# Output product one slot later, between the sixth and seventh transposition, and the first route weights transposed inside the first expert unit

## What is computed

```python
# x: 16 batches x 128 tokens x 128; y: 16 x 77 x 96; 16 heads of 8
q = layernorm(x) @ Wq.T + bq;  k, v = split(y @ Wkv.T + bkv)
att = softmax(q k / sqrt(8));  out = (att v) @ Wo.T + bo
x = x + tanh(g_xattn) * out
cur = layernorm(x)                       # 2048 tokens x 128
for r in range(4):                       # 4 rounds, 4 experts of width 512, top 2
    logits = cur @ Wg[r] + bg[r]
    cw = softmax over the best two of four, 0 for the others
    cur = cur + sum_e cw[e] * (gelu(cur @ W1[e] + b1[e]) @ W2[e] + b2[e])
x = x + tanh(g_ffn) * cur
```

## Time and profile before

| | |
|---|---|
| median of 3 runs (lowest, highest) | 456.02 us (455.89, 456.13) |
| the profiled execution | 455.4 us, of which its span 453.6 us |
| PE busy | 445.1 us, 98% of the span |
| DVE, ACT, POOL busy | 80%, 79%, 15% |
| granted TensorE clock | 1.000 over the span |
| slots 0 to 15 (12.1 to 85.6 us), the turn into the experts (to 96 us), expert units (the rest) | |

### The profile page before, as it was taken

The page is one execution under the profiler, slowest core; times in us unless marked ns, Lnnn a source line. Parts: engine busy times, 40 slices in busy tenths (PEclk is TensorE's granted clock), DMA queues, the critical chain, the costliest instruction groups (busy, mean ns, idle before and its releaser), DMA issues.

```text
span 453.6 us, 8799 instructions
## 1 busy us (share of the span) xinstructions
PE 445.1 (98%) x2856; PEld 354.8 (78%) x2856; DVE 362.1 (80%) x729; ACT 359.4 (79%) x742; POOL 70.2 (15%) x109
## 2 busy tenths in 40 slices
PE   8999999999999999999999999999999999999996
PEld 6666777778787888788878887888788878888885
DVE  6998989887978688868876888688768876887776
ACT  5777877696969779877987798779887888788883
POOL 7939884323000000000000000000000000000000
PEclk9999999999999999999999999999999999999999
DMA  6690000130021101300120022002200310023001
GB/s 168 194 206 15 1 10 10 61 129 3 0 93 30 66 1 36 153 0 1 72 117 1 1 80 108 0 2 100 88 0 1 135 53 1 0 95 117 25 0 46
DMA packets 12892, 25.18 MB, mean 56 GB/s; under 512 B 4615, under 2 KB 8496, under 8 KB 10800
## 3 DMA queue, kind: packets, MB, share of 16 engines
q1 hardware_dynamic: 9408, 22.23, 14.0%
q0 software_dynamic: 2784, 2.18, 2.6%
q10 hardware_dynamic: 656, 0.23, 0.2%
HBM read 22.82 MB, written 1.18 MB: 53 GB/s over the span
## 4 chain that ended last, share of the span: by engine, by line
PE 91%; DVE 4%; issue 2%; ACT 1%; DMA 1%; POOL 0%; SPq 0%; POOLq 0%; DVEq 0%
PE ps L1419 13%; PE ps L1421 13%; PE ps L1420 13%; PE ps L1408 12%; PE ps L1407 12%; PE ps L1406 12%; PE ps L1286 4%; PE ps L1308 2%; PE ps L1272 2%; PE ps L1314 2%; DVE least L899 1%; DMA x_sb<-in_x_dram 1%; PE ps L1373 1%; ACT g_sb L808 1%; PE ps L1321 1%
## 5 line engine op out<-in xcount | busy, mean ns | idle before, releaser
L955 DVE TENSOR_TENSOR h_lo<-g_sb,h_hi 128x512 fp32r<-128x512 f32 x256 | 169.9, 687 | 70.7 <-ACT h_hi L815 70.6
L808 ACT ACTIVATE g_sb<-ps,cols 128x512 f32<-128x512 f32 x256 | 174.4, 694 | 36.0 <-PE ps L1408 35.5
L815 ACT ACTIVATE h_hi<-g_sb 128x512 fp32r<-128x512 f32 x256 | 155.9, 640 | 0.0
L1419 PE MATMUL ps<-h_hi,w_hi 128*128 128x512 f32 x252 | 101.0, 401 | 0.1
L1406 PE MATMUL ps<-x_hi,w_hi 128*128 128x512 f32 x256 | 99.8, 390 | 0.0
L1408 PE MATMUL ps<-x_hi,w_lo 128*128 128x512 f32 x256 | 99.6, 389 | 0.0
L1407 PE MATMUL ps<-x_lo,w_hi 128*128 128x512 f32 x256 | 99.6, 389 | 0.0
L1421 PE MATMUL ps<-h_hi,w_lo 128*128 128x512 f32 x252 | 98.4, 390 | 0.0
L1420 PE MATMUL ps<-h_lo,w_hi 128*128 128x512 f32 x252 | 98.1, 389 | 0.0
L1419 PEld LDWEIGHTS ps<-h_hi,w_hi 128*128 128x128 f32 x252 | 47.3, 188 | 13.1 <-issue 2.7
L1408 PEld LDWEIGHTS ps<-x_hi,w_lo 128*128 128x128 f32 x256 | 48.1, 188 | 10.0
(11 more groups left out here) (126 smaller groups left out, 376.7 us busy)
## 6 DMA issues: line engine op xcount, KB each, us to landing
cwb_even<-cw_rows SPq DMA_DIRECT2D x8, 1024.0 KB, 5.4
cwb_odd<-cw_rows SPq DMA_DIRECT2D x8, 1024.0 KB, 4.7
w_hi<-in_L_ffn_W_dram POOLq DMA_DIRECT2D x2, 1024.0 KB, 10.3
w_in<-in_L_ffn_W_dram SPq DMA_DIRECT2D x1, 1024.0 KB, 5.4
x_sb<-in_x_dram SPq DMA_DIRECT2D x3, 256.0 KB, 5.3
out_dram<-xn SPq DMA_DIRECT2D x3, 256.0 KB, 2.5
ctxT<-in_ctx_dram SPq DMA_DIRECT2D x3, 115.5 KB, 5.1
v_st<-v_sb SPq DMA_DIRECT2D x14, 19.2 KB
```

The costliest lines, as they stand in the source:

```text
L808: nc.scalar.activation(g_sb[:, k, :], ps[:, k, :], ACT.Gelu_apprx_tanh, bias=b1_c[:, e * NF + k:e * NF + k + 1]).then_inc(gelu_done, 1)
L815: nc.scalar.activation(h_hi[:, u % 2, k, :], g_sb[:, k, :], ACT.Copy).then_inc(hi_done, 1)
L955: nc.vector.tensor_tensor(h_lo[:, u % 2, k, :], g_sb[:, k, :], h_hi[:, u % 2, k, :].bitcast(F32), ALU.subtract).then_inc(lo_done, 1)
L1419: mm(yb, w2_hi[:, w], hh, start=k == 0, stop=False)
```

## The change

Three edits. (1) The output product moves: PE computes `project_o(b-3)` in slot b, after the sixth transposition (after `transpose_probs(b, 1)`), instead of `project_o(b-2)` after the tenth; slot 15 holds both `project_o(12)` in the new place and `project_o(13)` in the old one. (2) DVE's `add_residual(b-3)`, which needs that product, moves from the start of slot b to behind `normalise_o(b-2)`; `add_residual(13)` moves to behind `weights(0)` in slot 15. (3) `transpose_weights(0)` moves from the end of slot 15 into `up(0)`, behind its first block, and its copy `move_cwT(0)` on ACT to behind `gelu(0, 0)`. Nothing is added or removed.

```diff
--- before.py
+++ after.py
@@ -286,7 +286,6 @@
 
         XT_AT = (10, 13)
         LG_AT = (13, 15)
-        CWT0_AT = 15
         ROUTER_SLOT = 15
         K_AT = {8: 3}
         V_AT = {10: 3}
@@ -320,12 +319,11 @@
                 next_job(("K", K_AT[b]), "act")
             if b in V_AT:
                 next_job(("V", V_AT[b]), "act")
-            if b == CWT0_AT:
-                next_job(("CWT", 0), "cwT")
             if b == 0:
                 job(("V", 2), "dve", 7)
                 job(("K", 2), "dve", 6)
                 last_early.update({6: ("K", 2), 7: ("V", 2)})
+        next_job(("CWT", 0), "cwT")
         next_job(("CWT", 1), "cwT")
         next_job(("XT", 2), "act")
         reads(("K", 0), "act")
@@ -784,9 +782,8 @@
                 exponentials(b, 1)
                 if b in XT_AT:
                     move_cur(XT_AT.index(b))
-                if b == CWT0_AT:
+                if b == ROUTER_SLOT:
                     gate(0)
-                    move_cwT(0)
                 if b in XN_AT:
                     move_xn(XN_AT[b])
                 if b in BUSY and b + 1 < B:
@@ -825,6 +822,7 @@
                 high(u, 3)
 
             gelu(0, 0)
+            move_cwT(0)
             gelu(0, 1)
             high(0, 0)
             gelu(0, 2)
@@ -1115,14 +1113,14 @@
             moments(0, 1)
             for b in range(B):
                 c, r = b // TC + 1, b % TC
-                if b >= 3:
-                    add_residual(b - 3)
                 if b >= 2:
                     invert_sums(b - 2)
                 if b + 1 < B:
                     smallest(b + 1, 1)
                 if b >= 2:
                     normalise_o(b - 2)
+                if b >= 3:
+                    add_residual(b - 3)
                 if b + 1 < B:
                     smallest(b + 1, 0)
                 if b + 1 < B:
@@ -1133,6 +1131,7 @@
                     moments(*MOMENTS[b])
                 if b == ROUTER_SLOT:
                     weights(0)
+                    add_residual(B - 3)
                 if b in NORMALISE:
                     normalise(NORMALISE[b])
                 if b == 0:
@@ -1158,7 +1157,6 @@
                     nc.vector.tensor_copy(wg_w[:, :, 0:E], wg_in[:, :, :]).then_inc(wg_split, 1)
             invert_sums(B - 2)
             normalise_o(B - 2)
-            add_residual(B - 3)
             weights(1)
             invert_sums(B - 1)
             normalise_o(B - 1)
@@ -1394,12 +1392,12 @@
                 tr(CWT(q), cw[:, 0:n, :, :].rearrange("p i e t -> p (i e t)"),
                    ident[:, :]).then_inc(job_mm if q < 2 else cwT_done, 1)
 
-            def up(u):
+            def up(u, blocks=range(NF)):
 
                 e, i = u % E, u // E
                 c = i % NC
                 pe.wait_ge(x_split, i + 1)
-                for k in range(NF):
+                for k in blocks:
                     w = slice(e * F + k * P, e * F + (k + 1) * P)
                     if u >= 1:
                         pe.wait_ge(gelu_done, NF * (u - 1) + k + 1)
@@ -1479,6 +1477,8 @@
                     scores(b + 1)
                 transpose_probs(b, 2)
                 transpose_probs(b, 1)
+                if b >= 3:
+                    project_o(b - 3)
                 if b in XN_AT:
                     transpose_xn(XN_AT[b])
                 if b in XT_AT:
@@ -1486,8 +1486,8 @@
                 if b in LG_AT:
                     logits(LG_AT.index(b))
                 transpose_probs(b, 0)
-                if b >= 2:
-                    project_o(b - 2)
+                if b == B - 1:
+                    project_o(B - 3)
                 if b in Q_AT:
                     project_q(Q_AT[b])
                 if b in K_AT:
@@ -1496,15 +1496,15 @@
                     project_v(V_AT[b])
                 if b >= 1:
                     weigh_values(b - 1)
-                if b == CWT0_AT:
-                    transpose_weights(0)
                 if b == 0:
                     project_v(2)
                     project_k(2)
             pe.wait_ge(w_split, 16)
             for h in range(2):
                 pe.wait_ge(below_done[h], B)
-            up(0)
+            up(0, range(0, 1))
+            transpose_weights(0)
+            up(0, range(1, NF))
             weigh_values(B - 1)
             transpose_weights(1)
             project_o(B - 2)
```

## The result

| | before | after |
|---|---|---|
| median of 8 runs each (lowest, highest) | 455.95 us (455.62, 456.23) | 457.38 us (457.21, 457.61) |
| span of the profiled execution | 453.6 us | 455.6 us |
| PE, DVE busy | 445.1, 362.1 us | 445.8, 363.6 us |

The change costs 1.43 us: ratio 1.0032, 95% interval 1.0021 to 1.0043. That is inside the range, on its slower side, and within 0.1 of rival B (457.3), not of the forecast (456.8).

What follows compares the result with a forecast made beforehand. The end was taken to hang on the chain from slot 14's sums through DVE's routers and ACT's list to `down(0)`'s third block, not PE. Slots -0.22 plus way +1.02 gave +0.80: median 456.8 us, range 456.0 to 457.6.

Steps and rivals of the forecast that it cites:

- rival B: Slots get slower too: additions between score reads cost a 0.25 signal, ACT-bound slots win nothing; +0.3, 457.3; chance 0.35.
- The way to `down(0)`: From slot 14's sums to the third block of `down(0)`: three delays arrive whole at PE, +1.02 us.
- (a): Slot 15: `add_residual(12)` before the router waits for the product after the sixth transposition; router starts 0.61 us later.
- (b): `add_residual(13)` moves from behind the second router to ahead of it, and nothing covers it: +0.26 us.
- (c): `move_cwT(0)` leaves ACT's slot 15 and enters its expert list between two `gelu`: +0.15 us.
- The slots: All slots up to slot 14: gains and losses from the moved product and additions sum to -0.22 us.
- Slots 2, 5, 8 and 9: Projection behind the tenth transposition waits for an ACT copy; 0.07 us can be won in each, four slots -0.27.
- Plain slots 6, 7, 12: DVE takes the place of ACT's wait; with a 0.20 us signal the next scores come 0.03 later per slot, +0.09 together.
- Slots 3 and 4: DVE is late; PE's 0.42 us wait for `oT_sb` goes but becomes a wait for `subtract`: scores +0.10 us.
- Slots 10 and 11: Same pattern as in slots 3 and 4, with DVE less late: +0.08 us.
- A: PE's time lands whole: slots are PE-bound, no wait follows, about -2.1 there, 454.9 in all, faster; chance 0.08.
- C: Routers not that late: product comes earlier or addition slips beside, 0.26 us instead of 0.61 in slot 15; 456.5; chance 0.15.

Runs made afterwards that it cites:

- second profile: The whole change run once more on another chip, same order of instructions, against the kernel before: 457.31 against 455.88 us, +1.43 (ratio 1.0027).
- slot 15 alone: Kernel before with product and additions in their new places only in slot 15, add_residual(13) ahead of router(1), no edit (3): 456.84 against 456.03 us, +0.81.
- shortened additions: Changed kernel with add_residual of batches 0 to 11 cut to 8 of 128 columns: 456.37 against 455.78 us for the kernel before, +0.59.
- slots 5 and 14: Kernel before with output product and addition in their new places in slots 5 and 14 only (batches 2 and 11): 455.52 against 455.88 us, -0.36.

## Why the prediction was right and wrong

**What bounds the kernel:** right. The sum of what moved before the third block of `down(0)`, 1.42 us in the second profile, is the measured 1.43, and what follows that block kept its length.

**The way to `down(0)`, forecast +1.02:** right, +1.02 and +1.03 in the two profiles. Terms (a) and (b), forecast 0.87: 0.87 in slot 15 alone and 0.88 with edits 1 and 2. Term (a) by itself: from the first transposition of slot 15 to the router 81.97 - 80.91 = 1.06 before and 83.53 - 81.87 = 1.66 after:

```profile
81.87 1.14 PE L1284 MATMUL ps<-ident,below 128*128 128x128 f32 x6 [0.28 <-ACT probT L723]
...
87.49 0.28 PE L1392 MATMUL ps<-ident,cw 128*16 128x128 f32 x1 [0.36 <-DVE lg L1001]
```

0.60 against the forecast 0.61. Term (b) 0.26 (86.80 to 87.06 on DVE), against 0.26. Term (c), forecast 0.15: 0.15 and 0.17. Edit (3)'s worth of nothing was right, and by the mechanism given: PE waits for the same late logits behind the first block (0.36 at 87.49).

**The slots, forecast -0.22:** wrong, +0.40 in two profiles (+0.24 where slot 4's stall is missing). This is where the missed 0.6 us lie; that the sum still fell inside the range is owed to the range, which took in case B. By term:

- *Slots 2, 5, 8 and 9*, forecast -0.27, measured -0.01, +0.04, +0.03, 0: +0.06 in all. It is the term that was sized most wrongly, by 0.33. The step that failed is "0.07 can be won": it took `xnT` as ready at the old time. But the product also stands ahead of the transposition of `xn`, and lasts as long as the wait that it fills. PE in the change, slot 5:

```profile
35.76 0.87 PE L1284 MATMUL ps<-ident,below 128*128 128x128 f32 x6
36.47 0.39 PE L1319 MATMUL ps<-wo_t,oT_sb 128*128 128x128 f32 x2
36.69 0.63 PE L1234 MATMUL ps<-ident,xn 128*128 128x128 f32 x4
```

and ACT:

```profile
37.36 0.60 ACT L695 ACTIVATE xnT<-ps 128x512 f32<-128x512 f32 x1
```

  `xnT` starts 37.36 - 34.99 = 2.37 after the scores, 36.53 - 34.19 = 2.34 before the change. Nothing in front of the last wait had become earlier, so nothing could be won behind it; 0.03 came on top. Slot 9 has no transposition of `xn`. There the projection does start 0.07 earlier, 2.29 us after the scores (56.11 - 53.82 in the second profile) instead of 2.36 (55.15 - 52.79), but it starts from a wait:

```profile
56.11 0.30 PEld L1248 LDWEIGHTS ps<-xnT,wq_t 128*128 128x128 f32 x2 [0.23 <-ACT probT L725]
```

  and `weigh_values` follows 1.06 behind it instead of 0.99, so that nothing is left.
- *Plain slots 6, 7, 12*, forecast +0.03 each, measured +0.04, +0.08, +0.07: +0.19 instead of +0.09. The step is "so I take 0.20": from the end of `subtract` to the scores it took 0.23 in slot 7 by the rows above, and the transpositions start 0.76 behind the scores instead of 0.73. Rival B's condition was a signal of over 0.22. That DVE takes the place of ACT's wait was right and is shown by the shortened additions; the addition's own cost was right too (0.27 from its start to the next instruction, 46.44 to 46.71, against 0.26).
- *Slots 3 and 4*, forecast +0.10, measured +0.10 with edits 1 and 2 alone, +0.25 to +0.26 in the three other profiles with both in the new order. The scores of slot 5, without edit 3 and in the change:

```profile
34.70 0.34 PEld L1275 LDWEIGHTS ps<-k_st,q_st 32*128 32x128 f32 x8 [0.33 <-issue]
```
```profile
34.99 0.34 PEld L1270 LDWEIGHTS ps<-k_st,q_st 32*128 32x128 f32 x8 [0.49 <-issue]
```

  What the further 0.16 us of "issue" are stays open: `subtract` ended 0.38 before the scores instead of 0.23, and no engine's end goes with them. The shortened additions, in the same new order, don't show them (4.55).
- *Slots 10 and 11*, forecast +0.08, measured 0 and +0.09. *Slot 13*, forecast -0.22, measured -0.20, and -0.23 where it alone was changed. *Slot 14*, forecast 0, measured 0. All right.

**The rivals.** B is nearest to what happened: nothing was won where ACT is waited for, and up to slot 14 it had +0.3, measured +0.24 to +0.40. Its signal of 0.25 did not come, only 0.22 to 0.23, at the very edge of its condition; and the upper part of the loss, slot 4's 0.16, is a stall that no case contained, so some of the nearness of its 457.3 is luck. It had 0.35 and the forecast 0.42: the forecast took a middle value for the signal between two bounds and went on with it as if it were known. A is out: the 0.22 us landed whole in one slot of twelve. C is out by slot 15 alone. "Slower by over 0.2%" had 0.43 and was the outcome.

**The signs.** The seventh transposition has no idle time before it: so. Plain slots 3.93 to 4.0: 3.98 to 4.02, with PE idle before the scores for 0.33, though the profile names no releaser where the forecast had DVE L906. The first router step 0.6 after `normalise_o`'s end, behind an addition that waits for PE: 83.53 - (82.63 + 0.29) = 0.61, with [0.34 <-PE ps L1319] before the addition:

```profile
82.63 0.29 DVE L922 TENSOR_TENSOR oT_sb<-ps,rT_sb 128x128 f32<-128x128 f32 x1
83.26 0.35 DVE L928 SCALAR_TENSOR_TENSOR x_sb<-ps,tgates,x_sb 128x128 f32<-128x128 f32 x1 [0.34 <-PE ps L1319]
```

ACT's `th` before the table load 0.65 later: not so. It is at 89.40, and without the later start (0.33) and slot 2's stall (0.22) it is 89.40 - 87.56 - 0.55 = 1.29 later; the 0.64 too much are what the slots were off by. The third block of `down(0)` at 96.8: at 98.03, of which 0.33 is the later start of that profile and 0.22 slot 2's stall.

## What to carry to other kernels

Work put into a wait of PE is only free if what it needs from the other engines is free too: here 0.22 us of PE per slot went into a real wait, and the addition that belonged to it moved from DVE's idle time into the stretch between two reads that the next slot waits for, where 0.12 us of it cost PE 0.13. Before a gain behind a wait is counted, ask what the waited-for work itself waits for: if the moved piece now stands ahead of it, the wait only moves. And where two bounds of a signal's cost decide the sign of several slots at once, give the case at the far bound its full weight.

## What the runs showed of the hardware

PE's way from a wait to its start was not the same everywhere. Before the scores, which wait for DVE and for ACT, it took 0.22 to 0.23 us in plain slots from the end of DVE's `subtract` to the first load; before `weigh_values` it took 0.12 from the end of `add_residual` in slot 7 of the change (46.79 to 46.91), and 0.14 in slot 15 before. That the second wait makes the difference is argued from the program and not shown: no run takes one of the two away.

PE also stalls now and then where the profile shows no wait for another engine: in slot 2's sums 0.22 to 0.73 us were lost in four of thirteen profiles (the first of the change, edit 3 alone, slots 5 and 14, and the shortened additions in the changed kernel, 6.31 us against 5.58), in two of which nothing was changed up to there. The last of these has a second one in slot 13, 0.52 us of "issue" before `weigh_values` where the change has 0.17, and its slot is 5.69 instead of 5.31. What makes these stalls stays open. One that stands in a single profile must not be costed as part of a change; a second profile and the median of the runs tell it apart. The profiled execution of the shortened additions took 456.90 us, the median of its runs is 456.37.
